# VectorE's rank chain of a unit in the third slot, apart from another unit's guess chain in the second

## The reference

```python
attn = jnp.einsum('bhnd,bhmd->bhnm', q, k) * SCALE
kth = jax.lax.top_k(attn, TOPK)[0][..., -1:]          # TOPK = 100 of 250
attn = jnp.where(attn >= kth, attn, -jnp.inf)
attn = jax.nn.softmax(attn, axis=-1)
out = jnp.einsum('bhnm,bhmd->bhnd', attn, v)
```

## Time and profile before

| | |
|---|---|
| timed runs | 2541.39 us median of 3 (2525.52 to 2543.54) |
| profiled execution | 2534.2 us, its span 2532.1 us |
| mean granted TensorE clock | 0.893 |

### The profile page before, as it was taken

The page is one execution under the profiler, slowest core; times in us unless marked ns, Lnnn a source line. Parts: engine busy times, 40 slices in busy tenths (PEclk is TensorE's granted clock), DMA queues, the critical chain, the costliest instruction groups (busy, mean ns, idle before and its releaser), DMA issues.

```text
span 2532.1 us, 41098 instructions
## 1 busy us (share of the span) xinstructions
PE 2282.6 (90%) x11650; PEld 1893.2 (75%) x11650; DVE 1758.0 (69%) x6138; ACT 1582.5 (62%) x5065; POOL 2.6 (0%) x13
## 2 busy tenths in 40 slices
PE   5768888899999999999899998888997899999999
PEld 2446767677787877877778777777886788888887
DVE  2339888999988998899998998988642333333332
ACT  1289988888877888888788887864331322333221
POOL 0000000000000000000000000000000000000000
PEclk9975568888988999899899998988996899999999
DMA  3000002221111122122121221212332112111111
GB/s 71 0 1 1 1 20 53 55 53 49 49 44 47 54 51 52 45 53 54 44 53 48 52 55 41 55 45 58 90 94 75 66 72 72 71 58 49 71 72 42
DMA packets 160058, 128.80 MB, mean 51 GB/s; under 512 B 24018, under 2 KB 150904, under 8 KB 159480
## 3 DMA queue, kind: packets, MB, share of 16 engines
q1 hardware_dynamic: 157244, 123.02, 17.9%
q10 hardware_dynamic: 2592, 3.33, 0.4%
HBM read 122.80 MB, written 3.46 MB: 50 GB/s over the span
## 4 chain that ended last, share of the span: by engine, by line
PE 49%; DVE 31%; ACT 11%; issue 6%; another core or an unknown queue 2%; DMA 1%; DVEq 1%; SPq 0%; ACTq 0%
PE bank L527 13%; PE bank L887 10%; PE bank L867 10%; ACT late L1012 5%; PE bank L641 3%; DVE late L1495 3%; DVE late L1357 3%; DVE late L1472 3%; DVE late L1475 3%; DVE late L1469 3%; DVE late L1465 2%; DVE late L1629 2%; PE bank L763 2%; PE bank L606 2%
## 5 line engine op out<-in xcount | busy, mean ns | idle before, releaser
L1012 ACT ACTIVATE late<-arena,late 125x250 bf16<-125x250 f32 x1152 | 565.8, 500 | 1.4 <-DVE late L1343 1.2
L527 PE MATMUL bank<-extra,wgu 128*128 128x250 f32 x1536 | 434.8, 433 | 1.6 <-issue 1.5
L1731 DVE TENSOR_TENSOR pair<-pair,arena 128x500 f32<-128x500 f32 x192 | 130.3, 679 | 372.6 <-PE bank L887 315.7
L527 PEld LDWEIGHTS bank<-extra,wgu 128*128 128x128 f32 x1536 | 323.3, 220 | 44.9 <-issue 5.2
L1186 ACT ACTIVATE pair<-bank 128x500 f32<-128x500 f32 x192 | 104.0, 585 | 328.9 <-PE bank L867 321.5
L641 PEld LDWEIGHTS bank<-vaug,late 125*125 125x125 f32 x1536 | 229.0, 223 | 98.7 <-ACT late L1023 76.5
L867 PE MATMUL bank<-xT,late 128*128 128x250 f32 (+1 forms) x1536 | 280.8, 388 | 0.0
L887 PE MATMUL bank<-late,pair 128*125 128x192 f32 x1536 | 273.3, 331 | 0.0
L641 PE MATMUL bank<-vaug,late 125*125 125x17 f32 x1536 | 228.4, 284 | 49.0 <-ACT late L1023 47.8
L606 PE MATMUL bank<-late 16*125 16x251 f32 x768 | 253.6, 456 | 16.7 <-ACT arena L989 15.7
L887 PEld LDWEIGHTS bank<-late,pair 128*125 128x125 f32 x1536 | 246.6, 187 | 26.0 <-issue 25.4
(11 more groups left out here) (189 smaller groups left out, 3706.9 us busy)
## 6 DMA issues: line engine op xcount, KB each, us to landing
arena<-d_comb_rows SPq DMA_DIRECT2D x64, 500.0 KB, 6.2
wdn<-in_b_d SPq DMA_DIRECT2D x192, 96.0 KB, 1.9
late<-comb_rows SPq DMA_DIRECT2D x128, 125.0 KB, 3.1
wgu<-in_b_g SPq DMA_DIRECT2D x192, 64.0 KB
wgu<-in_b_u SPq DMA_DIRECT2D x192, 64.0 KB
late<-comb_rows SPq DMA_DIRECT2D x128, 62.5 KB, 2.6
wgu<-in_b_g SPq DMA_DIRECT2D x192, 32.0 KB
wgu<-in_b_u SPq DMA_DIRECT2D x192, 32.0 KB
```

The source lines that it names most:

```text
L527: ins = pe.matmul(dst, lhs(t), rhs(t), start=t == 0, stop=t == 1)
L1012: ins = sc.activation(mk[:, n_par(u), t, :] if k == 3 else junk[:, t, :], s_sb[:, ub, t, 0:N], ACT.Sign, bias=thr[:, (n_par(u) + k + 1) % ...
L1731: dv.tensor_tensor(hid[:, s % 2, :, :], gl[:, s % 2, :, :], c, ALU.mult).then_inc(hid_set[1], 1)
```

## The change

The function `a_start_and_rank` stays as it is. It was called once in a period, in slot 1, for the unit started one period ago (u) and the one started four periods ago (r). Now it is called twice: in slot 1 for u alone, and in slot 2 for r alone. The second call stands at the same point of slot 2 as the first in slot 1: behind `m0_hidden`, ahead of the residual addition. In each call the waits between the steps are those for one chain, and each call settles and clears the step semaphore.

```diff
@@ -1701,8 +1701,10 @@
                 b = at_slot(T, END_AT - 1)
                 if b is not None:
                     add_experts(b)
-                if s == 1:
-                    a_start_and_rank(unit(i, g, p, 1), unit(i, g, p, 4))
+                if s == 1 and unit(i, g, p, 1):
+                    a_start_and_rank(unit(i, g, p, 1), None)
+                if s == 2 and unit(i, g, p, 4):
+                    a_start_and_rank(None, unit(i, g, p, 4))
                 if s == 3 and unit(i, g, p, 4):
                     a_flag(unit(i, g, p, 4))
```

## The result

The changed kernel takes **2652.9 us** (median of 4, 2644.8 to 2657.3) against 2542.5 (median of 4) for the kernel before: a ratio of **1.0443, 95% interval 1.0388 to 1.0498**. The direction and the mechanism are those of the main case (2613 us); the size is not: by the medians 72 us were forecast and about 111 measured; by the span of the profiled execution, for which the sum of the prediction was made, 76 us were forecast and 123.2 measured (2532.1 to 2655.3). The mean granted clock fell from 0.893 to 0.859. Every ratio here is taken over the fast runs alone and need not be the quotient of the two medians; the two differ by up to 0.3%.

The account below looks back on a forecast made before the run. The prediction took VectorE, in lock step with TensorE, as the bound. It added 31 us of unweaving and 45 us of waits at slot 0 to 2534.2, giving 2610, forecast as 2613 us; range 2520 to 2680, main case 2585 to 2655.

Parts of the forecast that it names:

- main case: Whole kernel: exposed latency on VectorE plus longer waits at slot 0, 2613 us, 2.8% slower; chance 0.47.
- Unweaving: VectorE's guess and rank chains, run apart, expose six dependent pairs of 0.11 us: 0.65 us per period, 31 us in all.
- Rival (d): On VectorE, running the two chains apart costs nothing; only the 45 us of waits stay, about 2583 us; chance 0.05.
- The new waits of TensorE: In slot 3, L617 waits for the rank chain some 4.5 us (g = 0), 3.5 (g = 1), about 3 (g = 2).
- With 6.8 us at half clock ... I take the third: TensorE behind the flag: VectorE's waits at slot 0 8.8 us per batch, taken as 7.3 against 3.9: 45 us.
- rival (c): TensorE's clock stays at half through slot 3: waits at slot 0 about 17 us per batch, about 2742 us; chance 0.08.
- Everything named above is held behind it: TensorE's slot 3: scores, down product, features, attention product and up product stand behind L617, which waits for the rank chain.
- Rival (a): Slots come into balance, clock stays up: waits at slot 0 shrink from 3.9 to 0.5 us per batch, about 2522; chance 0.18.

## Why the prediction was right in direction and too small

**Unweaving (31 us): right.** 0.65 us a period were forecast, 0.70 to 0.74 measured; alone it costs 35 us (1.0139). Rival (d), that it is free, is out. The rank chain took 2.33 us from first to last start, forecast about 2.4. What the six pairs and the second settling cost together is shown, not the share of each.

**The new waits of TensorE: right where placed.** L617 waits 4.63 us in g = 0, 3.75 in g = 1 and mostly 3.21 in g = 2, released by L1397; 4.5, 3.5 and about 3 were forecast. L754's wait fell to 1.00. L1626's wait rose by more than the forecast: from 57 to 152 us over the same batches, where about 100 was forecast.

**"With 6.8 us at half clock ... I take the third": the step that failed.** I forecast waits at slot 0 of 7.3 us per batch. From 600 us on they are about 12.3, 5.04 in nearly every g = 0, about 3.5 in g = 1 and 4.9 or 1.7 in g = 2. The half clock of the earlier trace rows, 6.8 us behind a wait of 3.02, was carried over as a fixed size; in g = 1 it fits (6.8 us at 0.53), in g = 0 the half clock went on through the small products of L763 to the end of slot 3, 13.4 us. There rival (c) was the nearest. From the flag to the end of the up product this gives 13.86 us in g = 0 against 7.3 at full clock, so 6.56 lost, where I had 2.9 (3.4 less 0.5). These 3.66 us are most of the 4.0 by which the wait of g = 0 was forecast too short (1.0, measured 5.04), and of the 5.0 per batch. In g = 2 the same wait of 3.21 us has both outcomes, so that a fixed size fails there too: 3.8 us at slot 0 in the mean, forecast 3.0. Summed over the run the waits at slot 0 grew by 89.8 us, forecast 45. All of it lies in the twelve batches from 400 to 1640 us (before) whose slots 0 go from 44.9 to 135.4 us, 3.7 to 11.3 per batch; the twelve other slots 0 (of 48), the first and the last ones, have some 27 us in both kernels, which is why the sum before is 72.8 and not 13.3 x 3.9 = 52. Two figures of the prediction do not come out as stated: the mean over the slots 0 is 3.7 per batch in those twelve batches and 4.5 over all 48, where it has 3.9; and with the whole of slot 3 at half clock its own terms give 18.7 per batch, where it has 17, so that rival (c) would be about 2765 in place of 2742.

**The flag as the cause: true, but not the only one.** "Everything named above is held behind it" describes the trace, and yet without it the time is the same (1.0400 with the guess moved in place of the rank; 1.0452 with the flag late, where part of the gain went into the late reading). VectorE's slot 2 is 2.4 us longer whatever is done with the flag, TensorE has begun its own slot 2 earlier, and its performer step of slot 3 needs the first operation of VectorE's slot 3. In the kernel before that step (L763 on L1607) waits three times, 1.0 us at most, in the stretch of the chain of waits; the prediction does not speak of it and should have asked what becomes of it.

**Rival (a): a real mechanism under a condition.** Its gain from even slots exists, and its condition was stated: the clock must be kept. With a filler in the idle time and the flag out of the way the time comes to 1.0016 in spite of the unweaving. Its limit, that it decides from a wait of some 2 us, did not hold: the clock fell behind single waits of 1.60 and 1.00 us too. Without filler and late flag the longer waits take the clock, as the argument against it said.

**Why the place decides.** Waits of TensorE ahead of slot 1 (guess in slot 0, 1.0170) or slot 2 (unweaving in slot 1, 1.0139, where the longest L754 wait is 3.8 us in place of 3.0) cost almost nothing beyond the unweaving. So much the runs show; the reason is read from the rows and was not tested by itself. Behind the wait of 3.02 us in slot 2 TensorE's work of the slot, at half clock, takes the 6.8 us from L754 to L627, and VectorE's slot 2 there lasts 8.3: it is covered. Behind the flag of slot 3 TensorE's work needs 7.3, 6.9 and 5.9 us at full clock, and VectorE has 9.8, 7.1 and 6.3 us of its own up to the operation that needs the tanh: half clock can't hide there in any of the three.

**What stays open.** Of the 51 us between the filler alone (1.0216) and the filler with the late flag (1.0016) the traces show the place: in the 36 slots 0 of the twelve batches VectorE waits 61.0 us with the first and 22.6 with the second, nearly all of the difference in g = 0, and 18 us less at slot 1. In the g = 0 shown for the filler alone, L769, the attention product and the up product take 4.28, 1.84 and 3.68 us, and at full clock 2.87, 1.02 and 1.96. These 3.95 us are about the 4.07 us that VectorE waits at the slot 0 behind them, so the clock, not the flag's hold, is the price there. What decides how long the half clock lasts is not shown: g = 0 and g = 1 differ in the wait and in the products, and g = 2 has both lengths with neither different.

## What to carry to other kernels

When work on one engine is moved between stages of a lock step, look at which engine has the cover in the stage *behind* the new place: 2 to 3 us of work added to the end of one slot cost nothing measurable here, and added to the end of another 3%. Before blaming one wait, list everything that the late engine releases there, since taking away the first gate can show a second, and check what reads the result that was made later. Two independent chains of small operations are worth weaving, 0.11 us for each dependent pair; and products that only fill idle time helped only where there was idle time, so they need a control in the other kernel. A stretch of half clock measured in one place is no constant for another: put a range on it.

## What the runs showed of the hardware beyond what I expected

The clock fell without a long wait. In the kernel with the filler in slot 2 the window from 1124.6 us has a granted clock of 0.51 for 6.8 us with TensorE busy in all of it; it begins within the 24 records of 34 columns (L768), behind a single wait of 1.00 us. With the filler ahead of the flag it fell within the same 24 records, behind a wait of 1.60 us. Behind the wait of 1.16 us in the earlier trace rows the up product took 1.86 us, its time at full clock. Behind equal waits of 3.21 us, with the same products following, the half clock lasted 3.4 us in one period and 10 in another. Seven products of 256 columns, 3.2 us, in place of a wait of 3.41 us kept it at 1.00 for the 9.7 us that I read, with the same small products in between.
